# Layer norm between attention passes: Newton steps and row scaling from VectorE to GpSimd, for four batches in step 3

## The reference

```
x = layernorm(x + self_attention(x))      # 16 heads, 8 key/value heads, rotary, all keys kept
x = layernorm(x + cross_attention(x, ctx))# 16 heads, causal over the first 512 context rows
x = layernorm(x + w3(silu(w1 x) * (w2 x)))# weights rounded to the 16 NF4 levels and scaled back
layernorm(t) = (t - mean(t)) / sqrt(var(t) + 1e-5)
```

## Time and profile before

| | us |
|---|---|
| three runs | 1101.43, 1103.11, 1104.53 |
| their median | 1103.11 |
| the profiled execution's own time | 1104.75 |
| its span, first to last instruction | 1103.0 |

### The profile page before, as it was taken

How to read it: one execution, slowest core, us unless ns; L and a number is a source line. 1 busy time by engine, 2 the same in 40 slices (tenths; PEclk the granted TensorE clock), 3 DMA queues, 4 the chain that set the end, 5 groups by cost and what they waited for, 6 DMA issues and landing times.

```text
span 1103.0 us, 17718 instructions
## 1 busy us (share of the span) xinstructions
PE 1034.4 (94%) x6280; PEld 671.7 (61%) x6280; DVE 754.0 (68%) x1684; ACT 488.4 (44%) x587; POOL 433.8 (39%) x462
## 2 busy tenths in 40 slices
PE   9999999999899988999889999999999999999995
PEld 7555555554555444556456565655647888888884
DVE  7789758566856689558776976896675645463635
ACT  3444344654465555546764765686451212111110
POOL 3558566986598444323342323333266000000000
PEclk9899899999999999999999999999999999999998
DMA  6741567386636864647576585747536203010021
GB/s 232 225 102 29 134 179 208 91 235 182 179 114 151 218 175 122 166 87 180 156 180 140 122 197 135 179 129 189 132 69 234 86 1 115 1 41 37 0 77 39
DMA packets 92618, 145.17 MB, mean 132 GB/s; under 512 B 22506, under 2 KB 39794, under 8 KB 92274
## 3 DMA queue, kind: packets, MB, share of 16 engines
q1 hardware_dynamic: 83218, 116.49, 40.5%
q0 software_dynamic: 8000, 26.75, 8.7%
q10 hardware_dynamic: 1312, 0.79, 0.3%
HBM read 78.09 MB, written 23.73 MB: 92 GB/s over the span
## 4 chain that ended last, share of the span: by engine, by line
PE 62%; DVE 19%; DMA 6%; issue 5%; POOL 3%; ACT 3%; SPq 1%; DVEq 0%; ACTq 0%; POOLq 0%
PE att_pv L1041 10%; PE att_pv L1298 7%; PE att_scores L1298 7%; PE att_scores_T L1328 7%; PE att_scores_T L1014 6%; PE att_scores L980 6%; PE att_scores_T L966 5%; PE att_scores_T L968 4%; PE att_scores_T L967 4%; DVE att_mx L1666 3%; DVE att_scores L1660 2%; DMA att_q_stack<-att_m_rows 2%; DVE att_nf_zone L1820 2%; DVE att_y L1716 1%; DMA att_nf_home<-nf_reciprocals 1%
## 5 line engine op out<-in xcount | busy, mean ns | idle before, releaser
L1469 ACT ACTIVATE att_probs<-att_scores_T 128x1024 f32<-128x1024 f32 (+2 forms) x256 | 218.9, 884 | 132.9 <-PE att_scores_T L1014 129.4
L1041 PE MATMUL att_pv<-att_probs,att_v 128*32 128x512 f32 (+3 forms) x1024 | 212.6, 531 | 1.6 <-POOL att_probs L843 1.4
L1666 DVE TENSOR_REDUCE att_mx<-att_scores 128x1 f32<-128x512 f32 x248 | 159.0, 683 | 79.0 <-PE att_scores L980 77.8
L1041 PE MATMUL att_pv<-att_probs,att_ones 128*32 128x512 f32 (+3 forms) x1024 | 212.5, 531 | 0.0
L980 PE MATMUL att_scores<-att_k_stack,att_q_stack 96*128 96x256 f32 (+1 forms) x504 | 173.6, 409 | 16.2 <-DVE att_mx L1666 7.4
L1014 PE MATMUL att_scores_T<-att_q_stack,att_k_stack 97*128 97x512 f32 (+2 forms) x512 | 143.1, 390 | 11.4 <-DVE att_nf_zone L1834 4.8
L1660 DVE CUSTOM_DVE_ANT_0 att_scores<-att_scores,att_cmask 128x128 f32<-128x128 f32 (+3 forms) x256 | 120.9, 511 | 40.3 <-PE att_scores L980 39.4
L843 POOL TENSOR_SCALAR_AFFINE_SELECT att_probs<-att_probs 128x256 f32<-128x256 f32 x128 | 58.1, 454 | 185.4 <-ACT att_probs L1469 182.0
L980 PEld LDWEIGHTS att_scores<-att_k_stack,att_q_stack 96*128 96x128 f32 x504 | 90.6, 194 | 64.3 <-DVE att_mx L1666 24.2
L1014 PEld LDWEIGHTS att_scores_T<-att_q_stack,att_k_stack 97*128 97x128 f32 x512 | 87.7, 195 | 53.2 <-DVE att_nf_zone L1834 18.0
L1559 ACT ACTIVATE att_probs<-att_scores 128x512 f32<-128x512 f32 x44 | 26.3, 598 | 207.4 <-PE att_scores L1298 207.4
(11 more groups left out here) (262 smaller groups left out, 2093.2 us busy)
## 6 DMA issues: line engine op xcount, KB each, us to landing
att_q_stack<-att_q_hi SPq DMA_DIRECT2D x128, 128.0 KB, 3.3
att_probs<-nf_x SPq DMA_DIRECT2D x28, 352.0 KB, 3.6
att_nf_home<-nf_reciprocals POOLq DMA_DIRECT2D x48, 176.0 KB, 4.8
att_q_stack<-att_q_lo SPq DMA_DIRECT2D x64, 128.0 KB, 3.6
att_k_stack<-att_k_hi SPq DMA_DIRECT2D x64, 128.0 KB, 3.5
att_nf_home<-nf_x SPq DMA_DIRECT2D x20, 352.0 KB, 3.6
w_nf<-att_nf_zone SPq DMA_DIRECT2D x192, 22.0 KB, 2.5
att_k_stack<-att_k_hi SPq DMA_DIRECT2D x64, 64.0 KB, 3.5
```

The costliest lines, as they stand in the source:

```text
L1041: last = T.matmul(pv[HD * j:HD * j + HD, sums, q0:S], lhs, pr[:, at:at + S - q0], start=(t == 0), stop=(t == TT - 1))
L1469: A.activation(probs_of(b, r)[:, 1024 * h:1024 * h + w], bank[:, 0:w], ACT.Exp, scale=SCALE).then_inc(st_free, 1)
L1666: V.tensor_reduce(mx[:, p % 2, TT * r + t:TT * r + t + 1], sco[:, r, :], AX.X, ALU.max).then_inc(sc_free, 1)
```

## The change

In all four cross-attention passes DVE does `aggregate` and `first_root` in step 3, copies the first guess, and signals `var_ok`. POOL then does three Newton iterations of four instructions each (twelve on 128x4 numbers, each waiting for the one before) and the four row scalings, behind the last mask of step 3; it signals `ln_ok`. In pass 7 `aggregate` and `first_root` move from (7, 6) to (7, 3). Where SP stores is unchanged.

```diff
+            roots = Chain(pool, pool_seq)
+            def root(b):
+                v, z, h = nwt[:, 0, :], nwt[:, 1, :], nwt[:, 2, :]
+                pool.wait_ge(var_ok, b - B + 1)
+                for i in range(3):
+                    if i > 0:
+                        roots.need()
+                    roots.tick(pool.tensor_tensor(h, z, z if i else h, ALU.mult))
+                    roots.need()
+                    roots.tick(pool.tensor_tensor(h, h, v, ALU.mult))
+                    roots.need()
+                    roots.tick(pool.tensor_scalar(h, h, -0.5, 1.5, ALU.mult, ALU.add))
+                    roots.need()
+                    roots.tick(pool.tensor_tensor(z, z, h, ALU.mult))
+                roots.need()
+            def scale_rows(ts):
+                for t in ts:
+                    last = pool.tensor_scalar(y[:, t, :], y[:, t, :], mv[:, t, 0:1], nwt[:, 1, t:t + 1], ALU.subtract, ALU.mult)
+                    if t < TT - 1:
+                        roots.tick(last)
+                    else:
+                        roots.need()
+                        last.then_inc(ln_ok, 1)
...
                         keep_causal(b, p, 2)
                         keep_causal(b, p, 3)
+                        if p == 3:
+                            root(b)
+                            scale_rows(range(TT))
...
-                    if crossed(b) and b < NB - 1 and p == 3:
-                        begin_spread(range(TT))
-                    if late(b) and b < NB - 1 and p == 3:
+                    if crossed(b) and p == 3:
+                        if b > B:
+                            dve.wait_ge(ln_ok, b - 1)
+                        aggregate(V, ch, mv, stats, nwt, range(TT))
+                        first_root(V, ch, mv[:, :, 1], nwt, nwi)
+                        ch.need()
+                        V.tensor_copy(nwt[:, 2, :], nwt[:, 1, :]).then_inc(var_ok, 1)
+                    if b == B - 1 and p == 3:
                         end_spread(range(TT))
-                    if b == B and p == 3:
-                        scale_rows(range(TT), TT - 1)
                     if b == B - 1 and p == 4:
                         scale_rows(range(2, TT), TT - 1)
-                    if (b, p) == (NB - 1, 7):
-                        scale_rows(range(TT), TT - 1)
-                    if quick and b > B and p == 5:
-                        scale_rows(range(0, 2), TT - 1)
...
-                    if quick and b > B and p == 5:
-                        scale_rows(range(2, TT), TT - 1)
...
-                    if (b, p) == (NB - 1, 6):
-
-                        spread(range(TT))
```

More of the change, by code:

```diff
@@ L400, in decoder_layer @@
         ln_ok, y_out, seq = sem("ln_ok"), sem("y_out"), sem("seq")
+        var_ok, pool_seq = sem("variances_ok"), sem("pool_seq")
         x0_in, x0_hi, x0_lo = [sem("x0_in0"), sem("x0_in1")], sem("x0_hi_ok"), sem("x0_lo_ok")
```

## The result

The changed kernel takes 1118.63 us (median of four runs, 1111.81 to 1121.34), the kernel before 1103.82 in the same comparison. The ratio is 1.0148, with a 95% interval of 1.0114 to 1.0182: slower by 15 us. The forecast was 1102.3 with a range to 1106.8, so it was wrong, and on the wrong side. The profiled execution took 1118.14, its span is 1116.4 against 1103.0.

What follows compares the result with a forecast made beforehand. PE, busy 94%, was taken to lose time waiting for DVE's comparisons and scaling behind the layer norm. Gains -6.8, pass 7 loss +5.4 and contention +0.6 gave -0.8 us: 1102.3 from 1103.11, 8-in-10 range 1097.8 to 1106.8.

Steps and rivals of the forecast that it cites:

- one term: POOL's four row scalings per pass: 0.63 us each, 2.5 together, upper 5.2, taken from rows of a cast and a product.
- POOL's layer norm: Root of 3.4 us plus scalings of 2.5 on POOL: 5.9 us a pass, lower end 5.0, upper 12.1.
- the room: POOL's time before PE asks for step 4's masks: 5.9 us and 4 more in (5, 4), 1.4 in (7, 4).
- Two signs of being wrong: (7, 4) wait, forecast 4.4 us, being over 7; stretches of passes 4 to 6 not shrinking by 5 us in all.
- Rival (b): POOL is dearer, so masks of (7, 4) come late and the kernel is slower: 1106 to 1108.5 us; chance 0.20.
- dear small instructions: Mechanism in Rival (b): twelve chained instructions at 0.45 plus 0.12 us take 6.9; (7, 4) wait 7.9, sum +2.7.
- dear scalings: Case in Rival (b): scalings on POOL at the two-input product's 1304 ns, sum +5.4 us.
- The gains: PE's shorter stretches: 2.70 us in (4, 3), 2.01 in (5, 5), 1.35 in (6, 5), 0.7 in (6, 6); together 6.8.
- The lower clock behind that wait: Slower PE clock behind the (7, 4) wait: 1.0 us added to the 4.4, a loss of 5.4.
- the 0.6 us of the sum: Contention: POOL's instructions hold up some of DVE's in passes 4 to 6, 0.2 us of PE time a pass.
- Rival (c): DVE's comparisons in (b, 3) wait for POOL's scalings, about 1 us more in each of passes 4 to 6: 1105.3; chance 0.09.
- A second step that failed: Claim that SP's earlier store in (7, 7) keeps nothing waiting; no cost was put in the sum.

Runs made afterwards that it cites:

- pass 7 as before: Changed kernel with pass 7's whole layer norm back on DVE in its old places; passes 4 to 6 keep the change: 1103.20 us, ratio 1.0016.
- no scaling: Changed kernel without the four row scalings, root still on POOL: 1101.04 us, ratio 0.9991; once more, 1101.50 us, ratio 0.9981.
- no iterations: Changed kernel without the twelve root instructions on POOL, the first guess scaling the rows: 1106.59 us, ratio 1.0031.
- four forms: Changed kernel with a different form of the scaling instruction on POOL in each of a pass's four tiles: 1111.35 us (one run).
- split: Changed kernel, but passes 4 to 6 do two of POOL's scalings in step 4 behind its masks, and pass 7 is as originally: 1101.52 us, ratio 0.9989.
- shared: Like split, but DVE does the other two scalings in step 4, before its comparisons in pass 4, behind them in passes 5 and 6: 1099.16 us, ratio 0.9963.
- mixed: Pass 4 as in shared, passes 5 and 6 as in split: 1098.52 us, ratio 0.9963.

## Why the prediction was wrong

**What failed** is one term: "A scaling reads one tensor of 512 columns: the cast's 628 ns is the nearest row, the two-input product's 1304 the upper end. I take 4 x 0.63 = 2.5 (upper 5.2)." A scaling took 2071 ns (mean of 16, 2064 to 2081), the four 8.25: above the end that was to bound it. The instruction is a tensor_scalar with two operations, and no row of POOL before had one on 512 columns. Cast and product were rows of other operations, and I took the number of tensors read for what sets the price. A bound must come from something dearer by a known reason; this one came from the next thing at hand. Why POOL takes that long for a tensor_scalar the runs don't show; that it does, they show in every pass and kernel that has one.

**What followed from it.** POOL's layer norm was to be 5.9 us (upper 12.1), and it is 11.7 in pass 7 and 13.0 in passes 4 to 6. In (7, 4) the wait was forecast at 4.4 and came at 10.13, and with the lower clock behind it the stretch grew by 11.3, not 5.4. In passes 4 to 6 the room, forecast at about ten, was no longer enough; "there POOL's work costs nothing in itself" became 2.1, 3.8 and 2.5 us in the three steps, 8.4 together. With the measured 11.7 and 13.0 the prediction's own working gives 11.7 - 1.4 = 10.3 and 13.0 - 9.9 = 3.1, and its sum becomes -6.8 + (10.3 + 1.0) + 3 x 3.1 + 0.6 = 14.4 us, where 14.8 were measured: the mechanism was right and a size was off. That the sum comes so near is in part luck, since its smaller terms missed both ways, as below. Two signs of being wrong that the prediction had named came true: the wait in (7, 4) is over 7 us, and passes 4 to 6 gained 5.9 in some steps and lost 8.4 in others, so they didn't shrink by 5. Rival (b), slower, had the right place and the masks behind POOL's work, but its named mechanism, dear small instructions, didn't come; its other case, dear scalings, did, with a product's 1304 as the highest price, so that its time ended at 1108.5.

**What was right.** The root in (7, 3): 3.4 us, 0.20 an instruction and 0.28 from start to start, as taken, while DVE has nothing but maxima beside it. The gains: (4, 3) by 2.84 (forecast 2.70), (5, 5) by 1.64 (2.01), (6, 5) by 0.54 (1.35, its two waits for DVE gone and one of 0.68 for a transfer in their place, in the rows above), (6, 6) by 0.92 (0.7): 5.9 where 6.8 were summed. That pass 7 is the place of the largest wait: the run with pass 7 as before shows it, some 15 us. The lower clock behind that wait: 1.15 (11.28 - 10.13), forecast 1.0.

**Contention** went both ways, and cost PE nothing that the rows show. In (4, 3) DVE's comparisons take 1.07 and 0.57 beside the root (rows below) where they took 1.08 and 0.58 before. Beside a scaling of POOL they do get longer: the first comparison of (4, 4), (5, 4) and (6, 4) takes 0.94, 0.91 and 0.94 in the changed kernel, where it takes 0.58 in each in the kernel without scalings. That is within the 0 to 0.63 that the prediction gave a collision, and PE has no wait for DVE of 0.3 us in those steps, so the 0.6 us of the sum isn't seen. The scalings themselves aren't held up: four take 8.25 to 8.27 in all passes. POOL's small instructions are, which I hadn't looked for. DVE's timeline in (4, 3) of the changed kernel:

```profile
520.28 1.07 DVE L1851 TENSOR_SCALAR att_nf_zone<-att_probs,att_nf_limits 128x1408 bf16<-128x1408 bf16 x2
522.53 0.57 DVE L1851 TENSOR_SCALAR att_probs<-att_probs,att_nf_limits 128x1408 bf16<-128x1408 bf16 x1
...
523.48 0.69 DVE L1622 TENSOR_TENSOR att_c_lo<-att_c_in,att_c_hi 128x512 fp32r<-128x512 f32 x1
```

POOL's in the same place:

```profile
520.45 0.46 POOL L871 TENSOR_TENSOR att_newton<-att_newton 128x4 f32<-128x4 f32 x1
520.99 0.42 POOL L873 TENSOR_TENSOR att_newton<-att_newton 128x4 f32<-128x4 f32 x1
521.50 0.19 POOL L875 TENSOR_SCALAR att_newton<-att_newton 128x4 f32<-128x4 f32 x1
...
522.62 0.53 POOL L875 TENSOR_SCALAR att_newton<-att_newton 128x4 f32<-128x4 f32 x1
...
523.58 0.65 POOL L871 TENSOR_TENSOR att_newton<-att_newton 128x4 f32<-128x4 f32 x1
```

The long ones coincide with DVE's comparisons and its subtraction of two tensors; those beside DVE's maxima stay at 0.20. That is 4.7 us for a root in passes 4 to 6 against 3.4, so 1.3 of the 13.0, and half of the waits of 2.6. Rival (c) falls: PE waits for no comparison of (4, 3), (5, 3) and (6, 3). The Trainium skill, SBUF — State Buffer, "Who interferes with whom", says that whoever issues first has the shared ports and the other is blocked; these rows agree with that rule in kind, as DVE's row starts first each time (520.28, 522.53, 523.48), and I had applied it in one direction only. That the lock is the cause was only read from the overlap, not tried.

**A second step that failed** is small: "In (7, 7) the store goes earlier; nothing there waits for it." The turned row of maxima (`att_m_rows`) behind 831.41 is late by 1.91 where it was 0.46 before, which is 1.45 us. ACT issues it, and with the rows ready early SP issues the store in the same place (timeline):

```profile
832.64 0.63 ACTq L1449 DMA_DIRECT2D att_q_stack<-att_m_rows  x1
832.76 0.43 SPq L578 DMA_DIRECT2D x_after_cross<-att_y  x1
```

All twelve profiled executions fall on one of two sides. In six the store is issued within 0.8 us of the row (changed kernel twice, no scaling twice, no iterations, four forms); there the row takes 4.1 to 5.0 us from its issue to PE's next matmul, and PE waits 1.73 to 2.68. In the six where DVE scales in (7, 7) the store comes 4.3 to 9.3 us behind the row; there it takes 2.7 to 3.0, and PE waits 0.27 to 0.54. That points to the store. How it holds the row up isn't shown, and no run moved the store alone.

**The measure.** But for the one slow run, runs of the kernel before went from 1095.7 to 1111.0 in these series, wider than the three that were known. In the profiled executions of these kernels the marker at the start of (4, 2), ahead of all that the change touches, stands between 500.3 and 509.0. The windows view of 100 to 200 us shows one reason: the same code at a granted clock of 0.97 in the kernel with pass 7 as before, and of 0.93 in split. The former:

```profile
100.00:200.00 100.00, 96.14 (x561) 52.54 (x561) 70.87 (x134) 46.51 (x53) 70.50 (x69) 0.97 0.65 165
```

And split:

```profile
100.00:200.00 100.00, 93.45 (x520) 51.74 (x513) 70.51 (x127) 43.75 (x50) 66.80 (x64) 0.93 0.62 161
```

Gains of 4 to 5 us therefore took twelve runs and more to be told from nothing, and one of 2 us wasn't told from it. The stretches show where a large wait lies, but those of one execution differ by some microseconds from those of the next.

## What to carry to other kernels

Before work moves to a slower engine, find a row of the same operation, with the same shape and type, on that engine; where there is none, measure it by itself, since the other terms of this prediction missed by 1.5 us or less each and that one decided. Then ask two things of the new place: how long the engine has until its next customer, which here gave the wait in (7, 4) to within half a microsecond for four durations, and what stands in a queue behind the result, as the next round's piece stood behind SP's late store. Two costs on one engine aren't to be priced one by one, either: in passes 4 to 6 root and scalings each fitted alone, and together they didn't. Part of the work may fit where the whole does not: with pass 7 left on DVE, four scalings on POOL in step 3 came out at a ratio of 1.0016 and two there with the other two in step 4 at 0.9989 (split), or 0.9963 where pass 4's other two are DVE's (shared, mixed); the change as made, with pass 7 on POOL too, at 1.0148.

## What the runs showed of the hardware

A tensor_scalar on GpSimd, 128x512 in fp32, takes 2.07 us with two factors a row, 1.94 with two constants and 1.61 with one factor and one operation, where the cast takes 0.63 and a tensor_tensor with a repeated column 1.04, less than one with two full tensors (1.29). DVE does two such scalings in 0.99. Dependent instructions on 128x4 numbers go every 0.28 us on POOL, and take 0.42 to 0.65 instead of 0.20 where DVE has begun a tensor_scalar on 128x1408 bf16 or a tensor_tensor on 128x512 just before; beside DVE's maxima they stay at 0.20. The other way round, such a tensor_scalar of DVE takes 0.90 to 0.94 instead of 0.58 when it falls into POOL's scalings, and these stay at 2.06 to 2.08. After a wait of PE of 10.13 us the granted clock was 0.50 for two microseconds and 0.58 for the next two, and `weigh` took 1.07 where it takes 0.62.
